# Two attentions and two feed-forwards on one core: input load, turned copies, latents and latent queries moved into the blocks that use them

## The reference

```python
x = L0_attn_hidden_states                      # 4 x 256 x 512 float32
x = layernorm(x + L0_attn(x))                  # latent attention: 32 heads, ranks 192 / 64, rope part of 64
x = layernorm(x + L0_ffn(x))                   # weights as 4-bit numbers with scales, hidden width 1376
x = layernorm(x + L1_attn(x))                  # 32 query heads, 8 key/value groups, plus 32 latent heads
x = layernorm(x + L1_ffn(x))                   # weights quantised to NF4 and back, hidden width 1376

# L0_attn, the part that the change moves:
c_q  = x @ w_q_down                            # 512 -> 192
c_kv = x @ w_kv_down                           # 512 -> 64, keys and values of all heads
k_rope = rope(x @ w_k_rope)                    # 512 -> 64
# L1_attn, the part that the change moves:
lq = x @ w_lq                                  # 512 -> 128; lk = lq @ w_lk and so on
```

## Time and profile before

| | us |
|---|---|
| median of 3 runs | 2628.86 (2627.57 to 2630.36) |
| profiled execution, whole | 2629.05 |
| its span from first to last instruction | 2627.3 |
| TensorE busy | 2360.2 (90%) |
| VectorE busy | 1761.5 (67%) |
| GpSimd busy | 1561.5 (59%) |
| ScalarE busy | 1471.7 (56%) |
| mean granted TensorE clock | 0.942 |

### The profile page before, as it was taken

The page is one execution under the profiler, slowest core; times in us unless marked ns, Lnnn a source line. Parts: engine busy times, 40 slices in busy tenths (PEclk is TensorE's granted clock), DMA queues, the critical chain, the costliest instruction groups (busy, mean ns, idle before and its releaser), DMA issues. The chain is left out here.

```text
span 2627.3 us, 44613 instructions
## 1 busy us (share of the span) xinstructions
PE 2360.2 (90%) x14333; PEld 2055.2 (78%) x14333; DVE 1761.5 (67%) x3131; ACT 1471.7 (56%) x3978; POOL 1561.5 (59%) x1320
## 2 busy tenths in 40 slices
PE   6799999996589958999999999999999999996998
PEld 5688888885368848889888888888888988885886
DVE  3366656664942227988888888888888888872132
ACT  1366656664033315766767667677676676674332
POOL 0646354631034428788787877878878878750442
PEclk7699989998579978999999999999999999998999
DMA  1201010101000011011110110111101111003000
GB/s 53 72 8 54 7 43 13 48 2 40 1 1 1 1 50 59 17 59 44 37 52 33 51 53 24 54 40 47 51 21 60 44 36 49 25 5 137 0 16 18
DMA packets 41301, 93.68 MB, mean 36 GB/s; under 512 B 4788, under 2 KB 6712, under 8 KB 39760
## 3 DMA queue, kind: packets, MB, share of 16 engines
q1 hardware_dynamic: 41044, 90.55, 10.3%
HBM read 79.78 MB, written 10.75 MB: 34 GB/s over the span
## 5 line engine op out<-in xcount | busy, mean ns | idle before, releaser
L1136 POOL TENSOR_TENSOR a_nf_acc<-a_nf_acc,a_nf_term 128x512 f32<-128x512 f32 (+1 forms) x416 | 586.1, 1409 | 143.3 <-ACT a_nf_term L1222 75.6
L1577 POOL TENSOR_TENSOR f_w_lo<-WGU,f_w_hi 128x512 fp32r<-128x512 f32 x88 | 112.8, 1285 | 358.5 <-ACT f_w_hi L1593 358.5
L1182 ACT ACTIVATE a_probs<-bank,a_dip 128x128 f32<-128x128 f32 (+1 forms) x512 | 208.7, 420 | 199.6 <-DVE a_dip L1433 199.6
L1191 ACT ACTIVATE a_probs<-a_probs,a_share 128x128 f32<-128x128 f32 (+1 forms) x512 | 191.8, 458 | 60.0 <-DVE a_share L1439 60.0
L1117 POOL TENSOR_TENSOR a_qk_lo<-a_straight,a_qk_hi 128x512 fp32r<-128x512 f32 (+1 forms) x160 | 194.2, 1215 | 31.3 <-ACT a_qk_hi L1168 31.3
L63 PE MATMUL bank<-a_wo_hi,a_ot_hi 128*128 128x512 f32 x512 | 212.1, 414 | 0.0
L1503 DVE TENSOR_SCALAR a_nf_term<-a_nf_unit 128x512 f32<-128x512 f32 (+1 forms) x288 | 204.4, 755 | 3.4 <-DVE a_nf_unit L1486 0.6
L1628 DVE TENSOR_TENSOR f_hidden<-bank,f_act_gate 128x512 f32<-128x512 f32 x44 | 30.5, 693 | 256.2 <-PE bank L65 240.4
L65 PE MATMUL bank<-a_wo_hi,a_ot_lo 128*128 128x512 f32 x512 | 201.0, 392 | 0.0
L64 PE MATMUL bank<-a_wo_lo,a_ot_hi 128*128 128x512 f32 x512 | 200.8, 392 | 0.0
L503 POOL TENSOR_TENSOR a_straight<-a_straight,a_crossed 128x512 f32<-128x512 f32 x64 | 82.4, 1288 | 191.4 <-DVE a_crossed L771 191.4
(11 more groups left out here) (247 smaller groups left out, 8603.1 us busy)
## 6 DMA issues: line engine op xcount, KB each, us to landing
a_raw<-in_l_o SPq DMA_DIRECT2D x64, 256.0 KB, 2.6
a_raw<-in_l_vk SPq DMA_DIRECT2D x32, 384.0 KB, 3.0
a_raw<-in_l_ql SPq DMA_DIRECT2D x32, 320.0 KB, 2.8
a_raw<-in_l_ou SPq DMA_DIRECT2D x32, 288.0 KB, 2.7
n_codes<-coded_w SPq DMA_DIRECT2D x8, 1056.0 KB, 12.6
a_raw<-in_l_nr SPq DMA_DIRECT2D x16, 384.0 KB, 2.9
a_nf_raw<-in_w_nf SPq DMA_DIRECT2D x24, 256.0 KB, 2.6
coded_w<-a_nf_acc SPq DMA_DIRECT2D x24, 256.0 KB, 2.1
```

What stands on the lines that cost most here:

```text
L1136: pool.tensor_tensor(acc, left, nf_term[:, i % CODE_RING, 0:w], ALU.add).then_inc(nf_added, 1)
L1182: act.activation(probs[:, n % 2, col:col + keys], bank[:, at:at + keys], ACT.Exp, bias=dip[:, n % 2, i:i + 1], accum_out=total[:, n % 2, i ...
L1191: ins = act.activation(cell, cell, ACT.Copy, scale=share[:, n % 2, i:i + 1])
L1577: pool.tensor_tensor(lo, src, hi.bitcast(F32), ALU.subtract).then_inc(part_lo[i], 1)
```

## The change

Seven blocks go: the loading block, the four of `transposed_block`, `latent_block` and `latent_query_block`. Their work is placed in the blocks that follow, cut into `turn_tile`, `high_tile` and `low_tile`.

- First attention: SyncE issues `ident`, X in four quarters with `w_down` after the first, the latents' tables, the attention's own tables, and goes on with the weight pieces. TensorE turns X, makes `W` 0 and 1, then the latents, waits for their last low half, and makes `W` 2 and 3 and `A` 0 and 1. VectorE sets the zero borders first, and splits `w_down` between turned tiles 1 and 2. The latents use the attention's own `straight` and `crossed`.
- Feed-forwards: the first four tiles are turned before unit 0, the other four between units 0 and 1, in banks 0 to 7. The first weights' split begins at once.
- Second attention: the last layernorm part, turned copies and latent queries stand at the head of each engine's list. SyncE starts with `w_lq` (into the space of `nf_term`) and goes on with tables and pieces.
- In both attentions VectorE does `probs_low(n - 1, 0)` before `out_low(n - 2)`.

```diff
+def turn_tile(pe, X, bank, ident, turned, t):
+    for k in range(KT):
+        last = pe.transpose(bank[:, k * P:(k + 1) * P], X[:, t, k:D:KT], ident[:, :])
+    last.then_inc(turned, 1)
+def high_tile(act, XT, bank, signals, flipped, t):
+    turned, hi_done, _ = signals
+    act.wait_ge(turned, TT * flipped + t + 1)
+    act.activation(XT.hi[:, :, t * P:(t + 1) * P], turned_view(bank), ACT.Copy).then_inc(hi_done, 1)
+def low_tile(dve, XT, bank, signals, flipped, t):
+    _, hi_done, lo_done = signals
+    at = slice(t * P, (t + 1) * P)
+    dve.wait_ge(hi_done, TT * flipped + t + 1)
+    dve.tensor_tensor(XT.lo[:, :, at], turned_view(bank), XT.hi[:, :, at].bitcast(F32), ALU.subtract)\
+       .then_inc(lo_done, 1)
...
@@ l0_attention_block, sync
+            sp.dma_start(ident[:, :], ident_d).then_inc(ident_landed, 16)
+            for i in range(TT // 2):
+                sp.dma_start(X[:, 2 * i:2 * i + 2, :], x[2 * i * P:2 * (i + 1) * P, :]
+                             .rearrange("(t p) d -> p t d", p=P)).then_inc(x_landed[i], 16)
+                if i == 0:
+                    sp.dma_start(lat_raw[:, :, :], w_down.rearrange("(k p) m -> p k m", p=P)).then_inc(lat_landed, 16)
+            sp.dma_start(lat_cos[:, :], lat_cos_d).then_inc(lat_landed, 16)
+            sp.dma_start(lat_sin[:, :], lat_sin_d).then_inc(lat_landed, 16)
@@ scalar
-                    for name in l0_units(True, False)[0:PAIRS + 2]:
+                    names = l0_units(True, False)[0:PAIRS + 2]
+                    for t in range(TT):
+                        high_tile(act, XT, banks[t % 4], signals, 0, t)
+                    for name in names[0:2]:
+                        unit_high(name)
+                    latents_high()
+                    for name in names[2:]:
                         unit_high(name)
@@ tensor
-            pe.wait_ge(tables_round, 2)
+            def latents():
+                pe.wait_ge(signals[2], TT)
+                pe.wait_ge(lat_w_ready, 1)
...
+            pe.wait_ge(ident_landed, 16)
+            for t in range(TT):
+                if t % 2 == 0:
+                    pe.wait_ge(x_landed[t // 2], 16)
+                if t >= 4:
+                    pe.wait_ge(signals[2], t - 3)
+                turn_tile(pe, X, banks[t % 4], ident, signals[0], t)
...
+                    for name in names[0:2]:
                         project(name)
+                    latents()
+                    pe.wait_ge(lat_ready, 1)
+                    for name in names[2:]:
+                        project(name)
+                    pe.wait_ge(tables_round, 2)
@@ vector
+            low_tile(dve, XT, banks[0], signals, 0, 0)
+            low_tile(dve, XT, banks[1], signals, 0, 1)
+            dve.wait_ge(lat_landed, 48)
+            dve.tensor_copy(lat_w.hi[:, :, :], lat_raw[:, :, :]).then_inc(lat_w_hi, 1)
+            dve.wait_ge(lat_w_hi, 1)
+            dve.tensor_tensor(lat_w.lo[:, :, :], lat_raw[:, :, :], lat_w.hi[:, :, :].bitcast(F32), ALU.subtract)\
+               .then_inc(lat_w_ready, 1)
+            for t in range(2, TT):
+                low_tile(dve, XT, banks[t % 4], signals, 0, t)
...
@@ vector, in the step of both attentions
                     shares(n)
+                    if not (first and n < 1):
+                        probs_low(n - 1, 0)
                     if not (first and n < 2):
                         out_low(n - 2)
                     if not (first and n < 1):
-                        probs_low(n - 1, 0)
                         probs_low(n - 1, 1)
@@ l1_attention_block, tensor
+            for t in range(TT):
+                pe.wait_ge(norm["x_ready"], TT + t + 1)
+                if t >= 4:
+                    pe.wait_ge(signals[2], 2 * TT + t - 3)
+                turn_tile(pe, X, banks[t % 4], ident, signals[0], t)
+            pe.wait_ge(lq_w_ready, 1)
+            pe.wait_ge(signals[2], 3 * TT)
...
+            pe.wait_ge(lq_ready, 2)
             pe.wait_ge(tables_round, 2)
@@ vector
+            measure(dve, X, norm, 1, late)
+            variance(dve, norm, 1, late)
+            low_tile(dve, XT, banks[0], signals, 2, 0)
+            normalise(dve, X, norm, 1, 1, late)
+            dve.wait_ge(lq_landed, 16)
+            dve.tensor_copy(lq_hi, lq_raw).then_inc(lq_w_hi, 1)
+            for t in range(1, 4):
+                low_tile(dve, XT, banks[t % 4], signals, 2, t)
+            dve.wait_ge(lq_w_hi, 1)
+            dve.tensor_tensor(lq_lo, lq_raw, lq_hi.bitcast(F32), ALU.subtract).then_inc(lq_w_ready, 1)
+            for t in late:
+                low_tile(dve, XT, banks[t % 4], signals, 2, t)
...
@@ ffn_block, scalar
-            for u, i in ((0, 0), (0, 1), (1, 0), (1, 1), (0, 2)):
+            split_high(0, 0)
+            for t in range(HT):
+                high_tile(act, XT, banks[t], signals, flipped, t)
+                if t == 1:
+                    split_high(0, 1)
+            deviation(act, norm, normed - 1, 1, late)
+            for u, i in ((1, 0), (1, 1), (0, 2)):
                 split_high(u, i)
+            for t in range(HT, TT):
+                high_tile(act, XT, banks[t], signals, flipped, t)
@@ tensor
+            for t in range(HT):
+                pe.wait_ge(norm["x_ready"], TT * (normed - 1) + t + 1)
+                turn_tile(pe, X, banks[t], ident, signals[0], t)
+            pe.wait_ge(signals[2], TT * flipped + HT)
             for u in range(UNITS):
                 at = slice(u // FT * HALF, (u // FT + 1) * HALF)
+                if u == 1:
+                    for t in range(HT, TT):
+                        pe.wait_ge(norm["x_ready"], TT * (normed - 1) + t + 1)
+                        turn_tile(pe, X, banks[t], ident, signals[0], t)
```

More of the change, by code:

```diff
@@ L362, in l0_units, with l0_attention_block @@
     return out
-def l0_attention_block(nc, X, CQ, KC, CV, norm, normed, ident, banks, w_nr, w_ou, cos_d, sin_d, mask_d):
+def l0_attention_block(nc, x, X, XT, CQ, KC, CV, signals, norm, normed, ident, ident_d, banks, w_down, lat_cos_d, lat_sin_d,
+                       w_nr, w_ou, cos_d, sin_d, mask_d):
     NP = 2
@@ L386, in l0_attention_block @@
         dip, total, share = sb("dip", [P, 2, 4], F32), sb("total", [P, 2, 4], F32), sb("share", [P, 2, 4], F32)
+        LN = QL + LAT + ROPE
+        lat_raw, lat_w = sb("lat_raw", [P, KT, LN], F32), pair("lat_w", [P, KT, LN])
+        lat_cos, lat_sin = sb("lat_cos", [P, SEQ], F32), sb("lat_sin", [P, SEQ], F32)
+        lat_units = [(at, h, rows) for at, rows in ((0, P), (P, QL - P), (QL, P)) for h in range(2)]
+        lat_dst = [lambda x, h: x[0][:, 0, h], lambda x, h: x[0][0:QL - P, 1, h], lambda x, h: x[1][:, h]]
         SA, SB_, TURN, AV = banks[0:4]
@@ L537, in _, with latents_high @@
         def _(act):
+            def latents_high():
+                for u, (_, h, rows) in enumerate(lat_units):
+                    hi = lat_dst[u // 2]((CQ.hi, KC.hi), slice(h * HALF, (h + 1) * HALF))
+                    if u < 4:
+                        act.wait_ge(lat_done, u + 1)
+                    else:
+                        act.wait_ge(lat_rotated, h + 1)
+                    act.activation(hi, banks[u][0:rows, :] if u < 4 else straight[:, h, :], ACT.Copy)\
+                       .then_inc(lat_hi, 1)
+                act.wait_ge(lat_done, 7)
+                act.activation(CV.hi[:, :, LAT:2 * LAT], banks[6][:, :].rearrange("p (t r) -> p t r", t=TT), ACT.Copy)\
+                   .then_inc(lat_hi, 1)
             def body(g, first, last):
@@ L1157, in _ @@
         def _(act):
+            high_tile(act, XT, banks[0], signals, 2, 0)
+            deviation(act, norm, 1, 1, late)
+            for t in range(1, TT):
+                high_tile(act, XT, banks[t % 4], signals, 2, t)
+            for h in range(2):
+                act.wait_ge(lq_done, h + 1)
+                act.activation(LQ.hi[:, h * HALF:(h + 1) * HALF], banks[h][:, :], ACT.Copy).then_inc(lq_hi_done, 1)
             def body(g, first, last):
@@ L1251, in _ @@
         def _(pe):
+            for t in range(TT):
+                pe.wait_ge(norm["x_ready"], TT + t + 1)
[4 more added lines that the diff above has]
+            pe.wait_ge(signals[2], 3 * TT)
+            for h in range(2):
+                for k in range(KT):
+                    last = product(pe, banks[h][:, :], (lq_hi[:, k, :], lq_lo[:, k, :]),
+                                   XT[:, k, h * HALF:(h + 1) * HALF], k == 0, k == KT - 1)
+                last.then_inc(lq_done, 1)
+            pe.wait_ge(lq_ready, 2)
             pe.wait_ge(tables_round, 2)
@@ L1392, in _ @@
         def _(dve):
+            measure(dve, X, norm, 1, late)
[10 more added lines that the diff above has]
+                low_tile(dve, XT, banks[t % 4], signals, 2, t)
+            for h in range(2):
+                dve.wait_ge(lq_hi_done, h + 1)
+                at = slice(h * HALF, (h + 1) * HALF)
+                dve.tensor_tensor(LQ.lo[:, at], banks[h][:, :], LQ.hi[:, at].bitcast(F32), ALU.subtract)\
```

(9 more changed lines are left out.)

253 lines of the change are left out of this document (72 added, 181 removed).

## The result

| | before | changed |
|---|---|---|
| median of the runs | 2628.81 (2627.57 to 2630.36) | 2588.12 (2582.9 to 2590.56) |
| profiled execution, whole | 2629.05 | 2582.9 |
| its span | 2627.3 | 2580.8 |
| TensorE busy | 2360.2 | 2364.9 |
| VectorE busy | 1761.5 | 1773.9 |

The ratio is 0.9837, 95% interval 0.9825 to 0.9848: 40.7 us less by the medians, 46.2 by the profiled executions (the changed kernel's was the shortest of its four). I had forecast 2558, range 2536 to 2581. The change gains what its direction promised and 30 us less than I said, and the time lies 7 us above my range.

What follows compares the result with a forecast made beforehand. Bound by block borders where TensorE waits for loads and splits, and by attention waits for `a_pt_lo`. -20.9 - 7 - 23.6 - 20 + 1 = -70.5 from 2629.05 gives 2558 us, range 2536 to 2581.

Steps and rivals of the forecast that it cites:

- Start of the first attention: Kernel start to first scores: loads issued together, GpSimd's pieces under the latents, scores at 73.5 instead of 94.46, -20.9 us.
- Feed-forwards: Both feed-forwards: unit 0 starts 5.4 us earlier, 16 transposes move between units 0 and 1; -3.5 us each, -7 together.
- Start of the second attention: Second attention's head: loads begin with the block, so A0 starts 23.6 us earlier, TensorE just in time; -23.6 us.
- My sum of 950.9, 8.4 and 1.7: Second attention's start: turned copies' end, latent queries, then halves and small copies; TensorE ready at 961.3, before A0 at 962.3.
- The `lq_lo` that I had 1.0 us late: Second attention's start: VectorE's sum beside GpSimd's splits is 1.0 us late, or by one split, total then 1 us higher.
- Reorder in the first attention: First attention's steps: `pt_lo` earlier, TensorE's second turn no longer 0.34 us late, 59 steps; -20 us, between 0 and -24.
- Reorder in the second attention: Second attention's steps: `pt_lo`'s lead doesn't add up, VectorE's idle time is mostly absorbed; +0.1 a group, +1 us.
- a projection, GpSimd's chain of sums and two peaks that waited for TensorE absorb nearly all: Second attention, 16-step group: these absorb nearly all of the 2.3 us delay from six steps, leaving +0.1 a group.
- My own bound (+18): Second attention's reorder, upper bound: all six delays of a group stay, 8 x 2.3 = +18 us.
- the rival of 2575 us: Second attention: VectorE's new idle time stays, 2558 + 17 = 2575 us; chance 0.17.
- the turns that are no longer held: Second attention: each held turn gains up to 0.57 us, bound -26; as the adding-up rival 2531 us, chance 0.12.

Runs made afterwards that it cites:

- both edits: Changed kernel with VectorE's old order in the second attention and that attention's loop 15 instructions later in TensorE's list: 2560.12 us (0.9727).
- shifted: Changed kernel with 30 already fulfilled waits (15 instructions) in TensorE's list ahead of the second attention's first projection: 2573.22 us (0.9776).
- the two best: Changed kernel, first attention's two middle groups unlooped; second attention with ACT's order turned too: 2550.34 us, or with VectorE's and ACT's old order: 2552.09 us.
- before, with 240 added: Kernel before with 480 already fulfilled waits (240 instructions) ahead of the 4-bit unpacking block's first product on TensorE: 2662.26 us against 2630.97 (1.0124).
- the kernel with ACT's order turned: Changed kernel, loop 15 instructions later, ACT's probs_high(n - 1, 0) ahead of out_high(n - 2) in the second attention: 2557.95 us (0.9727).
- the one with both attentions written out: Changed kernel, ACT's order turned in the second attention, middle groups of both attentions written one after the other instead of looped: 2554.26 us (0.9713).
- the kernel with only the second attention's groups written out: Changed kernel, VectorE's old order in the second attention, its six middle groups written one after the other instead of looped, every engine: 2560.85 us (0.9739).

## Why the prediction was wrong

**Start of the first attention: right** (-20.9 forecast, -21.2 measured), and by the steps that I gave. Timeline of the changed kernel, three engines:

```profile
11.48 0.83 DVE L667 CAST a_lat_w_hi<-a_lat_raw 128x1280 fp32r<-128x1280 f32 x1 [3.24 <-DMA a_lat_sin<-in_l_sin]
...
13.59 0.72 POOL L350 TENSOR_SCALAR a_wn_hi<-a_raw 128x512 fp32r<-128x512 f32 x1 [13.13 <-DMA a_raw<-in_l_nr]
...
16.77 0.42 PE L63 MATMUL bank<-a_wn_hi 128*128 128x64 f32 x1 [0.24 <-POOL a_qw_lo L358]
...
21.70 0.77 PE L63 MATMUL bank<-XT_hi,a_lat_w_hi 128*128 128x512 f32 x1
...
57.05 0.42 PE L63 MATMUL bank<-a_wn_hi 128*128 128x64 f32 x1 [1.41 <-DVE CV_lo L699]
...
73.30 0.45 PE L63 MATMUL bank<-KC_hi,a_q_hi 128*128 128x128 f32 x1 [4.85 <-POOL a_q_lo L373]
```

The latents' weights are there at 11.5 (12.0 forecast) and the first piece at 13.6 (14.2), so the loads did not get in each other's way; the latents follow `W` 1 without a gap at 21.70 (22.1); the tail, `W` 2 and 3 and A0 come as before, and the scores at 73.30 (73.5).

**Feed-forwards: right in kind, 1 us each too small** (-7 forecast, -9.2 measured). In the second one unit 0 comes 4.4 us into the block as said. The first `down` then follows after 14.8 us, 2 of which are the sixteen transposes, so units 0 and 1 take about 12.8 where they took 13.8. The granted clock of that stretch is 0.88, before 0.80: TensorE, which had stood for 3.85 us before unit 0, now stands for 2.3 and is back at 2.4 GHz sooner. In the first feed-forward unit 0 comes 5.1 us into the block, TensorE stands for 1.4 in place of 3.9, and the clock from unit 0 to the first `down` is 1.00, before 0.87. I had left the clock out of this term.

**Start of the second attention: right** (-23.6, measured -23.3). GpSimd's first split comes 8.0 us after SyncE's first issue, as forecast; TensorE was not late, A0 waited for `a_wql_lo`. (My sum of 950.9, 8.4 and 1.7 is 961.0, not 961.3; nothing hangs on it.) The `lq_lo` that I had 1.0 us late, the low half of the latent queries' weights, was not late (timeline of VectorE and GpSimd; its tile goes by the name `a_wo_lo`, whose space it uses):

```profile
903.56 0.68 DVE L1382 TENSOR_TENSOR a_wo_lo<-a_nf_term,a_wo_hi 128x512 fp32r<-128x512 f32 x1
903.90 1.03 POOL L1065 TENSOR_SCALAR a_wvk_hi<-a_raw 128x768 fp32r<-128x768 f32 x1 [19.84 <-DMA a_raw<-in_l_vk]
...
906.78 0.83 POOL L1065 TENSOR_SCALAR a_wvk_hi<-a_raw 128x768 fp32r<-128x768 f32 x1
```

The two did collide, and GpSimd paid: its first split took 1.03 us where the next took 0.83. With the old order in the first attention the split starts 0.04 behind `lq_lo` and takes 1.34, with both edits 0.44 behind it and takes 0.93. In all six kernels in which it starts more than 0.1 us before `lq_lo` ends, it ends 0.68 to 0.70 us after that end. The rule on the shared port from the Trainium skill, page "SBUF — State Buffer", section "Who interferes with whom", that one of the two waits until the other's instruction has ended, agrees with that; the one that came second waited here, and it was GpSimd and not VectorE. So this cost 0.2 us of GpSimd's time, in place of the 1 us that I had weighed for VectorE.

**Reorder in the first attention: right** (-20, measured -18.5). In a step of the changed kernel (timeline of VectorE and TensorE) the low half ends at 162.15 and the turn starts at 162.21, straight behind the last output product at 161.97, where it was 0.34 late before:

```profile
161.59 0.56 DVE L747 TENSOR_TENSOR a_pt_lo<-bank,a_pt_hi 128x384 fp32r<-128x384 f32 x1
...
161.97 0.40 PE L65 MATMUL bank<-a_bh_hi,a_ot_lo 128*128 128x512 f32 x1
...
162.07 0.41 DVE L752 TENSOR_TENSOR a_ot_lo<-bank,a_ot_hi 128x256 fp32r<-128x256 f32 x1
...
162.21 0.55 PE L588 MATMUL bank<-ident,a_probs 128*128 128x128 f32 x3
```

**Reorder in the second attention: wrong.** The step that failed is "a projection, GpSimd's chain of sums and two peaks that waited for TensorE absorb nearly all". I had found that VectorE idles longer before `pt_lo`, that the rotation behind it is late by that, and that six steps have nothing of their own to absorb it; then I let the places of slack count against steps in which they don't lie. A projection is no such place: it needs the bank which the late rotation gives back. The mean lengths of the steps over groups 1 to 5 (from one step's mask product to the next) name them:

| step of the group | 5 | 9 | 10 | 13 | 14 |
|---|---|---|---|---|---|
| before | 12.82 | 10.94 | 11.54 | 7.76 | 11.03 |
| changed | 13.24 | 11.35 | 12.04 | 8.21 | 12.01 |
| both edits | 12.67 | 10.94 | 11.52 | 7.76 | 11.05 |

That is 2.8 us a group, of which other steps give back about 1; over the eight groups three pairs of kernels, alike but for the reorder, differ by 11.8, 13.8 and 14.6. My own bound (+18) and the rival of 2575 us held this; the forecast itself was at the wrong end. And the other side, the turns that are no longer held, brought TensorE 7.6 us of waiting less over the whole span, since VectorE is the late one there.

**What no part of the prediction had: the second pause.** It costs 8.6 us (changed against shifted) to 10.6 (old order with and without the shift) of attention, and 12 to 15 by the medians. The 10.6 is not of the pause alone: with the old order and the pauses TensorE ran some 88 us of this attention at the low clock level, in the three others 55 to 60. The change shortened TensorE's list ahead of the loop; I had counted the pause behind a jump as part of the kernel before, and not asked on what it depends. Without this pause the changed kernel takes 2573.2 us, where the rival of the idle time that stays had 2575. With the pause and the old order it takes 2571.9. So either cause alone would have left the time inside the range; the range had room for the reorder, and this term stood nowhere in it. Both causes together make 26, and 2558 + 26 is 2584, beside the 2582.9 of the profiled execution.

## What to carry to other kernels

A wait that moves to the front of an engine's list moves all behind it: before putting a consumer earlier, look whether its producer on the other engine comes earlier too, and follow the delay to the next thing that the late engine hands back, step by step, without netting it against slack elsewhere. Where a profile has pauses with no releaser behind the jumps of a loop, any edit ahead of the loop can add or remove one; compare two variants only after looking at those pauses, and shift the loop if one has come. And before removing such a pause, look which engine catches up during it.

## What the runs showed of the hardware

**Where a loop begins in an engine's list decides how often the engine pauses behind its jump.** I counted TensorE's instructions ahead of the loop, a product as two (its weights' load and itself), took what is left after dividing by 256, and added how many instructions of the loop run before the second pause. The first count is of the program's list, the second of the records in the trace (sequencer's included, the first attention's loop once), good to one or two:

| kernels | start, by the list | start, by the trace | second pauses | place of the pause, list and trace |
|---|---|---|---|---|
| the two best | 137 | 101 | none | |
| changed; old order in either attention | 194 | 158 | 5 | 8 further: 202, 166 |
| all with 15 added | 209 | 173 | none | |
| before, with 240 added | 197 | 151 | 5 | 15 further: 212, 166 |
| before; before with the reorder | 213 | 167 | none | |

A loop that begins 8 or 15 instructions ahead of one place pauses there, and one that begins 7 or 1 behind it does not. By the trace that place is the same in both programs, 166; so the 10 by which the listed places differ must come from instructions in my list that have no record (the kernel before has seven blocks more, each with instructions that end it). It is also why I missed the place of the made pauses: by the list that loop began 3 behind the changed kernel's, by the trace 7 ahead of it, and the pause fell seven instructions later in the loop. The Trainium skill, page "Runtime: NRT & Kernel Launch", section "Instruction fetch mechanics", says that engines fetch their instructions in sequence in blocks of 256, and that a taken branch whose target is not at hand forces a fetch before execution can go on. The runs agree with it: a loop that begins 8 or 15 ahead waits twice, and one that begins 65 ahead (137, or 101 by the trace) waits once, so 65 instructions were enough for the next one to come in time. The page calls the crossing of a block's end mostly hidden; right behind a jump it cost 1.3 to 2.7 us here. That these places are block ends is inferred from the table, not seen.

**One such pause in the first attention costs far more than itself.** Its loop jumps once, the pause was 2.8 us, and written out the attention was 11 to 12 us shorter (520.1 to 521.1 against 532.0 and 532.2). The stretch behind the pause, in the looped kernel and in the one written out (columns as in the earlier trace rows):

```profile
332.00:346.00 14.00, 13.25 (x51) 11.67 (x52) 4.17 (x8) 3.97 (x14) 6.83 (x10) 0.51 0.15 43
```

```profile
325.00:345.00 20.00, 20.00 (x140) 17.33 (x139) 13.17 (x27) 13.11 (x43) 15.96 (x22) 1.00 0.23 61
```

Behind the pause TensorE runs at a granted clock of 0.51, the 1.2 GHz level, for some 14 us, as in the kernel before; without the pause the clock stays at 1.00. The first of these rows is of the kernel with ACT's order turned, the second of the one with both attentions written out. The length of the low stretch varies: 10 to 14 us in the changed kernel and its variants with this loop, whose first attention took 530.1 to 532.2, but some 3.4 us in the kernel with only the second attention's groups written out. Its pause was 2.7 us too, and its first attention took 526.8. So the pause with a short stretch at the low level costs some 6 us, and the longer stretch 3 to 5 more. Why the stretch is short in one kernel and long in the others, no run here tells.
